# Normalisation ahead of a scan in two rounds, and two score products on the row halves of TensorE

## The reference, cut to what matters

```
x = x + L0_conv(_gn(x))    # attention
x = x + L1_conv(_gn(x))    # scan along the width
x = x + L2_conv(_gn(x))    # attention
x = x + L3_conv(_gn(x))    # scan along the height
```

```
e1 = relu(w1 @ xf + b1)                 # 64 x 256
e2 = relu(w2 @ xf + b2)                 # 64 x 256
assembly = relu(w3 @ xf + b3)           # 512 x 256
attn = softmax(e1.T @ e2)               # scores 256 x 256
y = alpha * (xf @ attn.T) + assembly
```

## Time and profile before

| | |
|---|---|
| median of 3 runs | 296.87 us (296.14 to 297.03) |
| the profiled execution | 296.95 us, span 295.0 us |
| mean granted clock of TensorE | 0.988 |
| busy: PE, PEld | 270.6 us (92%), 230.9 us (78%) |
| busy: DVE, ACT, POOL | 168.8 us (57%), 72.1 us (24%), 51.8 us (18%) |
| the chain that ended last, by engine | PE 72%, DVE 13%, ACT 8%, issue 3% |

### The profile page before, as it was taken

The page is one execution under the profiler, slowest core; times in us unless marked ns, Lnnn a source line. Parts: engine busy times, 40 slices in busy tenths (PEclk is TensorE's granted clock), DMA queues, the critical chain, the costliest instruction groups (busy, mean ns, idle before and its releaser), DMA issues.

```text
span 295.0 us, 10767 instructions
## 1 busy us (share of the span) xinstructions
PE 270.6 (92%) x4527; PEld 230.9 (78%) x4527; DVE 168.8 (57%) x565; ACT 72.1 (24%) x162; POOL 51.8 (18%) x76
## 2 busy tenths in 40 slices
PE   6999999999958888888899999999999769999996
PEld 2688888886657877777785688878786669999996
DVE  2675454546646666666667865464647535555553
ACT  2135444433740000000000245635423820000000
POOL 0121000000302222222221140000000313333332
PEclk9999999999979999999999999999999979999999
DMA  7970000000000000000000000000000000002222
GB/s 238 414 292 3 0 0 2 1 0 0 2 0 0 0 0 0 1 0 0 0 0 2 0 0 2 0 1 0 2 0 0 2 1 0 0 0 71 69 67 78
DMA packets 4476, 9.21 MB, mean 31 GB/s; under 512 B 624, under 2 KB 3056, under 8 KB 3952
## 3 DMA queue, kind: packets, MB, share of 16 engines
q1 hardware_dynamic: 4176, 8.53, 7.8%
q10 hardware_dynamic: 288, 0.52, 0.6%
HBM read 6.96 MB, written 2.10 MB: 31 GB/s over the span
## 4 chain that ended last, share of the span: by engine, by line
PE 72%; DVE 13%; ACT 8%; issue 3%; DMA 1%; POOL 1%; DVEq 1%; ACTq 0%; POOLq 0%
PE bank L364 33%; PE bank L291 18%; PE bank L339 7%; ACT inb L446 5%; PE bank L303 5%; DVE state L664 4%; DVE lin L658 3%; PE bank L318 3%; PE bank L310 2%; ACT xn L420 2%; DVE st L485 2%; PE bank L266 1%; DMA x<-in_x 1%; DVE low L653 1%; PE bank L330 1%
## 5 line engine op out<-in xcount | busy, mean ns | idle before, releaser
L364 PE MATMUL bank<-state,wc 128*64 128x64 f32 x3840 | 126.3, 227 | 17.1 <-DVE state L664 13.3
L364 PEld LDWEIGHTS bank<-state,wc 128*64 128x64 f32 x3840 | 119.9, 141 | 24.0 <-DVE state L664 17.3
L291 PE MATMUL bank<-xn,w 128*128 128x256 f32 x256 | 60.5, 383 | 0.0
L291 PEld LDWEIGHTS bank<-xn,w 128*128 128x128 f32 x256 | 46.7, 190 | 7.2 <-issue 2.0
L646 DVE SCALAR_TENSOR_TENSOR state<-bank,negb,inb 128x64 f32<-128x64 f32 x116 | 29.2, 282 | 29.6 <-PE bank L364 24.5
L653 DVE TENSOR_TENSOR low<-bank,negb 128x128 f32<-128x128 f32 x60 | 17.3, 288 | 27.6 <-PE bank L364 22.4
L400 ACT ACTIVATE e<-bank,par 64x256 f32<-64x256 f32 x8 | 3.8, 469 | 111.3 <-PE bank L303 111.3
L339 PE MATMUL bank<-probT,xnT 128*128 128x256 f32 x128 | 29.5, 381 | 0.8 <-ACT rel L433 0.8
L339 PEld LDWEIGHTS bank<-probT,xnT 128*128 128x128 f32 x128 | 24.2, 190 | 4.7 <-ACT rel L433 1.6
L767 POOL TENSOR_TENSOR inb<-state,par 128x256 f32 x28 | 17.2, 615 | 54.0 <-DVE state L664 31.4
L266 PE MATMUL bank<-zeros 128*128 128x512 bf16 x87 | 24.0, 423 | 1.2 <-DVE zeros L710 1.2
(11 more groups left out here) (69 smaller groups left out, 198.4 us busy)
## 6 DMA issues: line engine op xcount, KB each, us to landing
w<-in_w SPq DMA_DIRECT2D x2, 1024.0 KB, 9.7
wc<-in_wc SPq DMA_DIRECT2D x2, 1024.0 KB, 12.8
result<-xh SPq DMA_DIRECT2D x15, 128.0 KB, 1.8
x<-in_x SPq DMA_DIRECT2D x3, 512.0 KB, 8.2
x<-in_x ACTq DMA_DIRECT2D x1, 256.0 KB, 4.4
x<-in_x SPq DMA_DIRECT2D x1, 256.0 KB, 4.2
w<-in_w ACTq DMA_DIRECT2D x1, 256.0 KB, 4.8
w<-in_w SPq DMA_DIRECT2D x1, 256.0 KB, 11.1
```

Of the source, the lines that this page charges most:

```text
L291: mm = nc.tensor.matmul(bank[2 + m // 2][:, m % 2 * POS:(m % 2 + 1) * POS], w3[l][:, k, m * P:(m + 1) * P], xn_s[:, k], start=(k == 0), st ...
L364: mm = nc.tensor.matmul(bank[units * h + v][c:c + TILE, (m - v * width) * COLS:(m - v * width + 1) * COLS], wc[l][:, k, m * P + c:m * P + ...
```

## The change

Three things are changed.

1. **Scan layers are normalised in two rounds.** Round 0 has the 12 columns of images 0 to 2 and is done inside image 3 of the attention layer in front: its group means behind the score products and its variances behind relu branch 1 on TensorE, the vector parts in the places where image 0 has those of its own layer. Round 1 has the 4 columns of image 3 and comes behind that image, between the same dummy products. GpSimd takes the power and forms nmr and bmr in both rounds; ScalarE's square root with its table loads and VectorE's refinement go.
2. **First states and inputs follow the rounds.** VectorE forms the first states of images 0 to 2 in image 3, behind its residual additions and ahead of its last sums; those of image 3 in four operations of 16 elements behind round 1. ScalarE writes 12 inputs at the end of image 3 and 4 behind round 1, and each has strips 1 to 15 instead of 2 to 15, so VectorE no longer makes strip 1. VectorE waits for all 16 ahead of step 0, no longer ahead of step 1.
3. **Scores.** e1 and e2 are written twice, on partitions 0 to 63 and 64 to 127 (four activations instead of two). The second score product uses the copies on 64 to 127. The products write two banks, the upper half of bank 0 and the lower half of bank 1, instead of both halves of bank 0.

The diff, cut to its core (`bank[b][:]` becomes `bank[b]` throughout):

```diff
+        pair01 = ctx.enter_context(nc.psum_tensor("banks01", [P, 2, 512], F32))
+        bank = [pair01[:, b] for b in range(2)] \
+            + [ctx.enter_context(nc.psum_tensor(f"bank{b}", [P, 512], F32))[:] for b in range(2, 8)]
+        scores = pair01.rearrange("p b c -> p (b c)")[:, 512 - POS:512 + POS]
...
-        e1 = sb("e1", [D, POS])
-        e2 = sb("e2", [D, POS])
+        e1 = sb("e1", [2 * D, POS])
+        e2 = sb("e2", [2 * D, POS])
...
         def norm_rounds(l):
-            return [(0, K), (K, NC)] if l in (0, 2) else [(0, NC)]
+            first = K if l in (0, 2) else NC - K
+            return [(0, first), (first, NC)]
...
-                    pe.wait_ge(s.e_ready, (n + 1) * 2)
+                    pe.wait_ge(s.e_ready, (n + 1) * 4)
                     for ic in range(PC):
-                        mm = nc.tensor.matmul(bank[0][:, ic * POS:(ic + 1) * POS],
-                                              e1[:, ic * P:(ic + 1) * P], e2[:], start=True, stop=True)
+                        rows = slice(ic * D, (ic + 1) * D)
+                        mm = nc.tensor.matmul(scores[:, ic * POS:(ic + 1) * POS],
+                                              e1[rows, ic * P:(ic + 1) * P], e2[rows], start=True, stop=True)
                     mm.then_inc(s.s_mm, 1)
                     if first:
                         group_means(l, 1)
+                    if last:
+                        group_means(l + 1, 0)
                     relu_branch(xn[h], 1, True)
                     if first:
                         group_variances(l, 1)
+                    if last:
+                        group_variances(l + 1, 0)
                     relu_branch(xn[h], 2, False)
...
-                first_norm(l)
+                critical_norm(l, 0)
                 attention(l)
-                first_norm(l + 1)
+                critical_norm(l + 1, 1)
                 scan_layer(l + 1)
...
-                    nc.scalar.activation(e1[:], bank[1][0:D, 0:POS], ACT.Relu,
-                                         bias=par[0:D, b12:b12 + 1]).then_inc(s.e_ready, 1)
-                    nc.scalar.activation(e2[:], bank[1][D:2 * D, 0:POS], ACT.Relu,
-                                         bias=par[D:2 * D, b12:b12 + 1]).then_inc(s.e_ready, 1)
+                    for rows in (slice(0, D), slice(D, 2 * D)):
+                        nc.scalar.activation(e1[rows], bank[1][0:D, 0:POS], ACT.Relu,
+                                             bias=par[0:D, b12:b12 + 1]).then_inc(s.e_ready, 1)
+                        nc.scalar.activation(e2[rows], bank[1][D:2 * D, 0:POS], ACT.Relu,
+                                             bias=par[D:2 * D, b12:b12 + 1]).then_inc(s.e_ready, 1)
...
                     if first:
                         normalise_next()
+                    if last:
+                        scan_inputs(l + 1, image_rows[l], 0, range(N - 1))
...
-            def scan_inputs(l, xr):
-                act.wait_ge(scan[l].bias, 1)
-                for n in range(N):
+            def scan_inputs(l, xr, r, ns):
+                act.wait_ge(scan[l].bias, r + 1)
+                for n in ns:
                     for k in range(K):
                         c = n * K + k
-                        nc.scalar.activation(inb[:, 2:, k, n * T:(n + 1) * T], xr[:, 2:, k, n * T:(n + 1) * T],
+                        nc.scalar.activation(inb[:, 1:, k, n * T:(n + 1) * T], xr[:, 1:, k, n * T:(n + 1) * T],
...
                     add_residual(2)
                     add_residual(3)
+                    if last:
+                        first_states(l + 1, image_rows[l])
                     for i, ms in enumerate(((0, 1), (2,), (3,))):
...
+            def first_states(l, xr):
...
+                dve.wait_ge(norm[l].done, 1)
+                nc.vector.tensor_tensor(strip(rest), strip(xr[:, 0]), wide(rstd), ALU.mult).then_inc(scan[l].scaled, 1)
+                dve.wait_ge(scan[l].scaled, 1)
+                nc.vector.tensor_tensor(strip(state[:, 0]), strip(rest), wide(nmr), ALU.add)
...
-                link(nc.vector.tensor_tensor(strip(rest[:]), strip(xr[:, 1]), wide(rstd), ALU.mult))
-                dve.wait_ge(s.bias, 1)
-                link(nc.vector.tensor_tensor(strip(inb[:, 1]), strip(rest[:]), wide(bmr), ALU.add))
...
+                dve.wait_ge(norm[l].done, 2)
+                for k in range(K):
+                    c = (N - 1) * K + k
+                    mm = nc.vector.tensor_scalar(state[:, 0, k, (N - 1) * T:], xr[:, 0, k, (N - 1) * T:],
+                                                 rstd[:, c:c + 1], nmr[:, c:c + 1], ALU.mult, ALU.add)
...
+                dve.wait_ge(s.inb, NC)
                 step(0, 1, 0)
-                dve.wait_ge(s.inb, NC)
...
             attention(0, AL_0)
-            set_variances(1, 0)
-            variances(1, 0)
-            inverse_std(1)
+            set_variances(1, 1)
+            variances(1, 1)
             scan_layer(1, xw, CB_1)
...
+            def input_bias(l, r, c0, c1):
+                cb = CB_1 if l == 1 else CB_3
+                pool.wait_ge(norm[l].done, r + 1)
+                nc.gpsimd.tensor_tensor(bmr[:, c0:c1].rearrange("p (n k) -> p n k", k=K),
...
+                    .then_inc(scan[l].bias, 1)
...
                         .then_inc(s.done, 1)
+                    if l in scan:
+                        input_bias(l, r, c0, c1)
...
             inverse_std(0)
+            inverse_std(1)
             scan_layer(1, xw, CB_1)
             inverse_std(2)
+            inverse_std(3)
             scan_layer(3, xh, CB_3)
```

More of the change, by code:

```diff
@@ L265, in keep_warm @@
                 for _ in range(count):
-                    nc.tensor.matmul(bank[7][:], zeros[:, 0:P], zeros[:], start=True, stop=True)
+                    nc.tensor.matmul(bank[7], zeros[:, 0:P], zeros[:], start=True, stop=True)
             def group_means(l, r):
@@ L519, in variances @@
                                      .rearrange("p (c s) -> p c s", s=SETS), AX_X).then_inc(s.gvar, 1)
-            def inverse_std(l):
-                s = norm[l]
-                dve.wait_ge(s.std, 1)
-                link(nc.vector.reciprocal(inv[:], root[:]))
-                link(nc.vector.scalar_tensor_tensor(half[:], inv[:], -0.5, gvar[:], ALU.mult, ALU.mult))
-                link(nc.vector.tensor_tensor(err[:], half[:], inv[:], ALU.mult))
-                nc.vector.scalar_tensor_tensor(rstd[:], err[:], 1.5, inv[:], ALU.add, ALU.mult).then_inc(s.rstd, 1)
             def normalise_first(l):
@@ L545, in image @@
                     dve.wait_ge(s.xnT_mm, n * PC + 2)
-                    nc.vector.tensor_copy(xnT[:, 1], bank[7][:]).then_inc(s.xnT_copied, 1)
+                    nc.vector.tensor_copy(xnT[:, 1], bank[7]).then_inc(s.xnT_copied, 1)
                     dve.wait_ge(s.s_mm, n + 1)
-                    nc.vector.reduce_max(mx[:], bank[0][:].rearrange("p (c j) -> p c j", c=PC), AX_X)\
+                    nc.vector.reduce_max(mx[:], scores.rearrange("p (c j) -> p c j", c=PC), AX_X)\
                         .then_inc(s.chain, 1)
@@ L562, in image @@
                         variances(l, 1)
+                    if last:
+                        variances(l + 1, 0)
                     def add_residual(m):
@@ L605, in chunks @@
                     return slice(u * width, (u + 1) * width)
-                def first_scaled(u):
-                    nc.vector.tensor_tensor(strip(rest[:, chunks(u)]), strip(xr[:, 0, chunks(u)]), wide(rstd)[:, chunks(u)],
-                                            ALU.mult).then_inc(s.scaled, 1)
-                def first_state(u):
-                    dve.wait_ge(s.scaled, u + 1)
-                    nc.vector.tensor_tensor(strip(state[:, 0, chunks(u)]), strip(rest[:, chunks(u)]),
-                                            wide(nmr)[:, chunks(u)], ALU.add).then_inc(s.state[u], 1)
-                dve.wait_ge(norm[l].rstd, 1)
-                nc.vector.tensor_tensor(nmr[:], gneg[:], rstd[:], ALU.mult).then_inc(norm[l].done, 1)
-                for u in range(units):
-                    first_scaled(u)
-                dve.wait_ge(norm[l].done, 1)
-                for u in range(units):
-                    first_state(u)
-                for u in range(units):
-                    dve.wait_ge(s.state[u], 1)
-                link(nc.vector.tensor_tensor(strip(rest[:]), strip(xr[:, 1]), wide(rstd), ALU.mult))
-                dve.wait_ge(s.bias, 1)
-                link(nc.vector.tensor_tensor(strip(inb[:, 1]), strip(rest[:]), wide(bmr), ALU.add))
+                dve.wait_ge(norm[l].done, 2)
[3 more added lines that the diff above has]
+                                                 rstd[:, c:c + 1], nmr[:, c:c + 1], ALU.mult, ALU.add)
+                    if (k + 1) % width == 0:
+                        mm.then_inc(s.state[k // width], 1)
                 def product(u, h):
@@ L748, in scan_layer @@
                 bias = par[:, cb:cb + K].unsqueeze(2).to_broadcast([P, K, COLS])
```

(5 more changed lines are left out.)

57 lines of the change are left out of this document (21 added, 36 removed).

## The result

The changed kernel took 285.91 us, median of four runs (285.46 to 287.02), against 296.95 of the kernel before beside it: the ratio is 0.964 (95% interval 0.9617 to 0.9664). Forecast were 287.5 us with a range of 285.7 to 290.2. The number lies inside, 0.2 above the lower end, and beside rival B's 285.8; that it fell so near to B is in part luck, as the last part shows.

A forecast was written before the change was run, and what follows sets the result against it. TensorE's queue was taken to bound attention, and each scan start to lose twice, by the wait for ScalarE's inputs and the slow clock behind it. 296.87 - (3.68 + 4.44 + 1.26) = 287.5 us, range 285.7 to 290.2.

The forecast's parts named there:

- rival B: Attention scores: the pair of score products overlaps whole, 0.43 us saved instead of 0.21 per image, 285.8 us; chance 0.13.
- What bounds the kernel: At both scan starts, the wait for ScalarE's inputs (2.59, 3.12 us) and TensorE's slow clock (1.09, 1.32 us) would go.
- The score products: In attention, the two products on row halves take three lengths instead of four: 0.21 us saved per image.
- A: The forecast itself, 287.5 us, with its own bounds of 286.8 to 288.4; chance 0.62.
- The two more activations: ScalarE's four activations ahead of the attention scores end half a microsecond early, at 59.74, so the added two cost nothing.
- The early round: Attention's last image: normalising 12 columns delays what follows by 0.24 us; VectorE doesn't wait; twelve inputs end at 74.5.
- First states ahead of the last sums: Two VectorE operations in attention's last image, 0.77 us; sums start 0.58 us later in layer 0, 0.91 in layer 2.
- The late round: Between attention and scan: from M, the product of group means, to step 0 of the scan takes 5.83 us.
- The sum: Whole kernel: 3.68 us (scan 1) + 4.44 (scan 3) + 1.26 (scores) = 9.38 off 296.87, giving 287.5 us.
- C: Attention scores: the row halves bring nothing, 1.7 us less gained, 289.2 us; chance 0.12.
- D: TensorE's clock falls at both scan starts all the same: 2.4 us less gained, 289.9 us; chance 0.10.
- E: Wait moves whole ahead of step 0 of each scan, all sixteen inputs late: 4.9 us slower, 301.8 us; chance 0.03.

The follow-up runs named there:

- before_dummies: Kernel before with 16 dummy products behind TensorE's second scan step, the wait left in place: 294.91 us, ratio 0.9949.
- halves_only: Kernel before with the score part alone (four activations, two row halves, two banks): 293.98 us, ratio 0.9916.
- strip_one: Changed kernel with strip 1 of image 3 written by VectorE, step 0 waiting only for twelve inputs, 9 dummies instead of 11 before each scan: 286.51 us.

## Why the prediction was right, and where it was off

- **What bounds the kernel**: right. The waits of 4.20 and 5.03 us for ScalarE's inputs are gone, down to 1.44 ahead of each step 0, all but about 0.2 of it beside TensorE's product, and so is the slow clock behind them. `before_dummies` measured the clock's part alone, 2.4 us in its profile for a forecast of 2.41. This is one execution's price: `halves_only` has the same gap once with the slow clock behind it and once without.
- **The score products**: the step that failed. "The order is first product, both passes, then second product, both passes" gave three lengths, 0.21 us saved; measured are two lengths and 0.43, since two records start within 6 ns of each other from the beginning, where that order has the second product one pass behind. Over eight images that is 1.8 us more than forecast. The rule that I set beside it, the Trainium skill's span model ("TensorE: Matmul & The Clock Gate", part 3), gave the 0.43: here the trace agrees, 0.63 us to the next instruction instead of 1.06. The scan's own matmuls, 33 ns each, had spoken for it, and I had set them aside because they follow each other without end and the pair stands alone. The chances, 0.62 for A and 0.13 for B, leaned the other way.
- **The two more activations**: right, ready 0.55 us early.
- **The early round**: right. The 12 inputs run from 68.35 to 74.19; this image began 0.34 us later, so in the forecast's times that is 68.01 (forecast about 68.35) to 73.85 (74.5). Nobody waits for GpSimd.
- **First states ahead of the last sums**: over-sized, by three terms in layer 0 (and nearly the same in layer 2). With the pair's whole overlap TensorE's delay was 0.02 us instead of 0.24, the residual pair took 0.71 instead of 0.79 to the next operation and the two states 0.66 instead of 0.77: 0.41 together. The wait of 0.43 that the sums had in front was in the forecast's 0.58. The group means are 0.17 and 0.51 us later than before, counted from the image's start, where 0.58 and 0.91 were forecast.
- **The late round**: M + 5.64 to step 0 for a forecast of 5.83 (bmr's hand-over 0.28, not 0.35; four inputs in 2.03). The scan's first four steps in layer 3 took 7.25 us instead of 7.48.
- **The sum**: 1.27 + 4.28 + 1.28 + 5.26 = 12.1 us of work for a forecast of 9.4. 1.8 of the 2.7 is the pair, the rest the small terms above (states, late round, first steps of layer 3). The medians are 11.0 apart. Of the 1.1 between, 0.57 us lies outside the span; the other 0.5 is, by estimate, the head: spans of about 283.4 at the median and 271.3 from the first product on put that product at 12.1, where the profile of before had 11.60. Why either is so, is open. So the 285.9 lies beside B's 285.8 by luck in part: B with the small terms as measured is 284.9, and what the prediction didn't have, the head and the time outside the span, adds 1.1.
- **The rivals**: B came true as a mechanism, C and D didn't, and E is real: 300.4 us when brought about, for 301.8 by my sum. The sum still had the pair at 0.21; against the kernel before beside it, it is 4.5 us slower, where E said 4.9, and 3.2 with the pair at 0.43.

## What to carry to other kernels

Where an engine waits in a place where TensorE stands too, price the wait and the slow clock behind it by separate terms; dummy products in the gap measure the second and leave the first (4.12 us of VectorE's wait with them, 4.20 without). Work that a later stage needs can be split by what is known early, even if the last part's latency stays: twelve of sixteen inputs moved under existing work were worth far more than the second round cost. And a pair of products with a contraction of 64, here two in float32 with a bank each, ran in the time of one once the second had a copy of its operands on the other half of the partitions (0.63 us to the next instruction instead of 1.06), made by an engine that had the time.

## What I had not expected of the hardware

- Two float32 products on different row halves start 6 ns apart in each of their passes; cut in pieces and issued in either order they do so in pairs, 6 to 14 ns apart.
- Operations of VectorE on 16 elements with a scalar for each partition take 0.29 us in the changed kernel (0.89 us for four with their overlap), and 0.49 as `strip_one`'s second four in layer 1 and 0.37 in layer 2, with GpSimd at work beside them. Whether GpSimd is the cause wasn't tried.
- The same gap of 3.8 us in TensorE's work took the clock to 1.2 GHz in the first scan and left it at 2.4 in the second (`halves_only`), where the kernel before had 1.2 in both.
- The head: eleven dummy products took 2.53 us in one execution (`before_dummies`) and 4.60 in another, and the first image starts anywhere from 10.47 to 13.35 us.
